# A fused two-layer kernel: u and v rows turned and moved apart with v first, the first pair's rows turned by TensorE, an earlier first gate, ScalarE in the opening normalisation, and two batches in one round of TensorE's loop

## The reference, cut to what matters

```python
xn = layernorm(x)
x = x + L0_attn(xn) + L0_ffn(xn)
xn = layernorm(x)
x = x + L1_attn(xn) + L1_ffn(xn)

def L0_attn(xn):                         # 16 channels of rank 64
    u, v = xn @ fu.T * s, xn @ fv.T * s  # (tokens, 16 x 64) each
    F = einsum("csr,ctr->cst", u, v); q = sigmoid(F)
    g1 = einsum("cst,ctr->csr", q, v); g2 = einsum("cst,csr->ctr", q, u)
    return (g1 @ fu + g2 @ fv) * s
```

## Time and profile before

| | |
|---|---|
| median of 3 runs | 1467.37 us (1465.08 to 1467.95) |
| the profiled execution | 1468.4 us, its span 1466.6 us |
| opening, router, experts | 0 to 158 us |
| batch 0, without layer 1 | 158 to 302 us |
| batches 1 to 7 of the loop | 302 to 1413.8 us |
| tail | 1413.8 to 1466.6 us |
| busy, of the span | PE 95%, DVE 62%, ACT 47%, POOL 3% |

### The profile page before, as it was taken

One profiled execution on the slowest core, in us unless ns is written; L12 is line 12 of the kernel. 1 busy time (PEld: TensorE's weight loads), 2 busy tenths in 40 slices (PEclk: granted clock), 3 DMA queues, 4 the chain that ended last, 5 costly groups with the idle time before them and its releaser, 6 DMA issues.

```text
span 1466.6 us, 24503 instructions
## 1 busy us (share of the span) xinstructions
PE 1389.9 (95%) x7806; PEld 793.9 (54%) x7806; DVE 903.6 (62%) x1559; ACT 688.9 (47%) x1058; POOL 44.1 (3%) x41
## 2 busy tenths in 40 slices
PE   6999798899998999999999999999999999999968
PEld 3566444455564555555565555555655555555534
DVE  8868443366655665656655656556555666566657
ACT  3556344444443544454444543454544454454421
POOL 4000400000000000000000000000000000000000
PEclk9999899999999999999999999999999999999988
DMA  6012222112221212221112211221212111221110
GB/s 207 1 31 66 43 35 31 26 29 35 30 30 31 33 27 30 36 32 31 26 26 39 36 29 24 36 34 28 30 29 36 32 26 27 38 30 27 25 30 8
DMA packets 302620, 51.37 MB, mean 35 GB/s; under 512 B 280545, under 2 KB 300769, under 8 KB 302465
## 3 DMA queue, kind: packets, MB, share of 16 engines
q1 hardware_dynamic: 302128, 47.82, 19.4%
q0 software_dynamic: 336, 1.64, 0.3%
HBM read 11.64 MB, written 4.19 MB: 11 GB/s over the span
## 4 chain that ended last, share of the span: by engine, by line
issue 85%; DVE 1%; PE 1%; POOL 1%; ACT 0%; POOLq 0%; DVEq 0%
PE psum L1231 1%; DVE arena L917 0%; DVE arena L923 0%; DVE arena L915 0%; POOL u_w_hl L608 0%; POOL v_w_hl L608 0%; POOL rstd_s L623 0%; POOL up_hl L608 0%; DVE arena L939 0%; PE psum L1575 0%; DVE xn_s L663 0%; POOL u_w_hl L605 0%; POOL v_w_hl L605 0%; DVE x_all L932 0%; POOL up_hl L605 0%
## 5 line engine op out<-in xcount | busy, mean ns | idle before, releaser
L1172 ACT ACTIVATE arena<-psum 128x1024 f32<-128x1024 f32 x504 | 476.0, 1030 | 636.5 <-PE psum L1231 636.3
L1231 PE MATMUL psum<-arena 128*64 128x512 f32 x2016 | 466.0, 605 | 26.0 <-DMA arena<-blocks 14.6
L1231 PEld LDWEIGHTS psum<-arena 128*64 128x64 f32 x2016 | 135.0, 138 | 290.0 <-issue 244.7
L1231 PE MATMUL psum<-u_parts,v_parts 64*128 64x512 f32 x1536 | 199.5, 404 | 11.9 <-issue 11.2
L1231 PE MATMUL psum<-v_parts,u_parts 64*128 64x512 f32 (+1 forms) x1568 | 201.9, 397 | 0.0
L866 DVE TENSOR_SCALAR o_hl<-psum,sums 128x512 fp32r<-128x512 f32 x126 | 94.4, 749 | 162.1 <-PE psum L1231 162.1
L1231 PEld LDWEIGHTS psum<-u_parts,v_parts 64*128 64x128 f32 x1536 | 141.7, 187 | 93.1 <-issue 45.3
L1231 PEld LDWEIGHTS psum<-v_parts,u_parts 64*128 64x128 f32 (+1 forms) x1568 | 145.3, 184 | 81.5 <-issue 51.1
L868 DVE SCALAR_TENSOR_TENSOR o_hl<-psum,sums,o_hl 128x512 fp32r<-128x512 f32 x126 | 94.6, 751 | 4.5
L1121 ACT ACTIVATE arena<-psum 128x512 f32<-128x512 f32 x128 | 77.1, 625 | 18.5 <-PE psum L1231 18.5
L923 DVE TENSOR_TENSOR arena<-psum,arena 128x512 f32<-128x512 f32 x96 | 64.6, 689 | 33.7 <-PE psum L1231 31.7
(11 more groups left out here) (211 smaller groups left out, 1517.0 us busy)
## 6 DMA issues: line engine op xcount, KB each, us to landing
arena<-blocks SPq DMA_DIRECT2D x1008, 32.0 KB, 2.0
x_all<-in_x SPq DMA_DIRECT2D x4, 512.0 KB, 5.4
upper<-in_we SPq DMA_DIRECT2D x8, 256.0 KB, 2.7
expert_rows<-upper SPq DMA_DIRECT2D x16, 128.0 KB, 2.5
xn_s<-expert_rows SPq DMA_DIRECT2D x8, 256.0 KB, 2.9
out<-x_all SPq DMA_DIRECT2D x8, 256.0 KB, 2.5
arena<-in_e POOLq DMA_DIRECT2D x1, 896.0 KB, 5.7
arena<-in_wi POOLq DMA_DIRECT2D x1, 576.0 KB, 5.7
```

The source lines that it names most:

```text
L1172: nc.scalar.activation(th_of(un), psum[:, at:at + 2], ACT.Tanh, scale=0.5 * FACTOR_SCALE ** 2).then_inc(s_th, 2)
L1231: return nc.tensor.matmul(out, lhsT, rhs, start=start, stop=stop)
```

## The change

Five edits.

1. **u and v apart, v first.** `turn` is called twice, for `v_raw` and then `u_raw`, 128x512 each, with buffers (`v_blocks`, `u_blocks`) and semaphores of their own. SP moves v with 16 DMAs of 16 KB and then u with 16 more, so 32 for a pair. `weighted` waits for v's at unit 0 and for u's only at unit 4 (half o = 1).
2. **First pair's rows by PE.** The turn of pair 1 of batch 0 and its 16 DMAs go; PE turns `u_raw` and `v_raw` with four transposes each (`prep` with k = 3 and 4), between the last expert's steps, and ACT copies the banks (`prep_tok`). PE now waits for these copies before its first scores (`s_prep_free` 8 in place of 6).
3. **First gate.** The steps gate 0 and up 0 move from half 5 to half 3, behind `v`; in the tail likewise.
4. **ACT's half of the opening.** ACT normalises every odd batch (`odd_rows`, four instructions of 128x128), DVE makes for it the shift and keeps the even ones. The router logits come in pairs of batches, two matmuls of 32 columns each, and the exponential is two instructions on 32 partitions each.
5. **Two batches a round on PE.** PE's loop `Fori(1, B)` becomes batch 1 written out and `Fori(1, B // 2)` with two batches in its body. DVE, ACT and SP keep one batch a round.

The core of the diff:

```diff
-FULL_STEPS = {1: [("back", 0)], 2: [("norm", 0)], 3: [("kq", 0), ("v", 0)], 12: [("down", 0)], 15: [("yo", 0), ("yo", 1)]}
-FULL_STEPS |= {h: [("gate", f), ("up", f)] for h, f in ((5, 0), (6, 1), (9, 2))}
+FULL_STEPS = {1: [("back", 0)], 2: [("norm", 0)], 3: [("kq", 0), ("v", 0), ("gate", 0), ("up", 0)], 12: [("down", 0)], 15: [("yo", 0), ("yo", 1)]}
+FULL_STEPS |= {h: [("gate", f), ("up", f)] for h, f in ((6, 1), (9, 2))}
...
+    return 3 + k if is_first(g) else g * 2 + 5 + k
+
+
+def moved_count(i, j):
+
+    return (i + (j > 0)) * MOVED
...
+            def move_blocks(blocks, tok, moved):
+
+                for r in range(QUARTERS):
+                    for a in range(QUARTERS):
+                        sp.dma_start(tok[32 * r:32 * r + 32, :, 32 * a:32 * a + 32],
+                                     blocks[32 * a:32 * a + 32].rearrange("t (k r c) -> t k r c", k=TB, r=QUARTERS)[:, :, r])\
+                          .then_inc(moved, 16)
+
+            def move_tokens(i, j):
+
+                sp.wait_ge(s_vb, i * PAIRS + j)
+                move_blocks(v_blocks, v_tok[:, (j + 1) % 2], s_vt[j])
+                sp.wait_ge(s_ub, i * PAIRS + j)
+                move_blocks(u_blocks, u_tok[:, (j + 1) % 2], s_ut[j])
+
             for j in range(1, PAIRS):
-                move_tokens(0, j, later_blocks)
+                move_tokens(0, j)
...
             def part_rows(h):
                 dve.wait_ge(s_rstd, h + 1)
-                for n in range(h * X_PART, (h + 1) * X_PART):
-                    if n >= 2:
-                        dve.wait_ge(s_xT, n - 1)
-                    normalised(xn_g[:, n % 2], n, mv1[:, n, :, 0:1], rstd1[:, n].unsqueeze(2)).then_inc(s_xn, 1)
+                odd, even = h * X_PART + 1, h * X_PART
+                nc.vector.scalar_tensor_tensor(shift1[:, odd], mv1[:, odd, :, 0], -1.0, rstd1[:, odd], ALU.mult, ALU.mult)\
+                  .then_inc(s_shift, 1)
+                if h:
+                    dve.wait_ge(s_xT, even - 1)
+                normalised(xn_g[:, 0], even, mv1[:, even, :, 0:1], rstd1[:, even].unsqueeze(2)).then_inc(s_xn, 1)
...
+            def turn(i, j, raw, blocks, turned, moved):
+
+                if not (isinstance(i, int) and i == 0 and j == 1):
+                    dve.wait_ge(moved[(j - 1) % PAIRS], moved_count(i if j else i - 1, (j - 1) % PAIRS))
+                nc.vector.transpose(blocks[:], raw[:]).then_inc(turned, 1)
...
-                        turn(i, j, later_blocks)
+                        turn(i, j, v_raw, v_blocks, s_vb, s_vt)
+                        turn(i, j, u_raw, u_blocks, s_ub, s_ut)
...
+            def odd_rows(n):
+                act.wait_ge(s_shift, n // 2 + 1)
+                if n >= 2:
+                    act.wait_ge(s_xT, n - 1)
+                for k in range(TB):
+                    ins = nc.scalar.activation(xn_g[:, 1, k], x_all[:, n, k], ACT.Identity, bias=shift1[:, n, k:k + 1],
+                                               scale=rstd1[:, n, k:k + 1])
+                ins.then_inc(s_xna, 1)
+
+            odd_rows(1)
+            for n in range(0, B, 2):
+                transposed(n, 0)
+                transposed(n + 1, 1)
+                if n + 3 < B:
+                    odd_rows(n + 3)
...
+            def prep_tok(k, tok, bk):
+                act.wait_ge(s_prep_full, prep_index(0, k) + 1)
+                copy(tok[:, 1].rearrange("p k c -> p (k c)"), bk[:]).then_inc(s_prep_free, 1)
...
+            prep_tok(3, u_tok, bank[2])
+            prep_tok(4, v_tok, bank[3])
...
+            def logits(pair):
+                pe.wait_ge(s_xnT, 2 * pair + 2)
+                for g in range(2):
+                    ins = mm(bank[2][g * 64:g * 64 + 32], wr_b[:, pair * 32:pair * 32 + 32], xn1T[:, 2 * pair + g],
+                             pair == 0, pair == B // 2 - 1)
+                return ins
...
+                else:
+
+                    pe.wait_ge(s_prep_free, prep_index(g, k - 2) + 1)
+                    for t in range(TB):
+                        ins = nc.tensor.transpose(bk[:, t * P:(t + 1) * P], (u_raw if k == 3 else v_raw)[:, t * P:(t + 1) * P],
+                                                  ident[:])
...
+                if blk == 0 and isinstance(i, int) and i == 0 and j == 1:
+                    pe.wait_ge(s_prep_free, prep_index(0, 4) + 1)
+                elif blk == 0:
+                    pe.wait_ge((s_vt, s_ut)[o][(j - 1) % PAIRS], moved_count(i if j else i - 1, (j - 1) % PAIRS))
...
             prep(0, 2, 1, 0, bank[1])
             probabilities_back(*last)
+            prep(0, 3, 1, 0, bank[2])
             attend(*last)
+            prep(0, 4, 1, 0, bank[3])
             expert_out(*last)
...
             iteration(0, True, False)
-            with pe.Fori(1, B) as i:
-                iteration(i, True, True)
+            iteration(1, True, True)
+            with pe.Fori(1, B // 2) as m:
+                for n in range(2):
+                    iteration(m * 2 + n, True, True)
             iteration(B, False, True)```

How the instructions stand, at the three places that matter. First SP, from the last expert to the first pairs of batch 0, before (`expert_rows<-upper` are the experts' stores, `xn_s<-expert_rows` their loads for the scatter):

```order
L514 DMA expert_rows<-upper 64x4x128 x4
L533 DMA arena<-arena 32x8x32 x16
L514 DMA expert_rows<-upper 64x4x128 x2
L542 DMA xn_s<-expert_rows 128x4x128
L533 DMA arena<-blocks 32x8x32 x32
L542 DMA xn_s<-expert_rows 128x4x128
L533 DMA arena<-blocks 32x8x32 x80
```

More of the change, by code:

```diff
@@ L231, in scatter_bank @@
         def scatter_bank(i):
-            return x_bank(("sc", 0), not isinstance(i, int))
+            return x_bank(("sc", 0), not (isinstance(i, int) and i == 0))
         x_all = sb("x_all", [P, B, TB, D])
@@ L375, in build @@
         w_hl = [u_w_hl, sb("v_w_hl", [P, 2, PAIRS * D], F32R)]
-        later_blocks = sb("blocks", [P, 2, T])
+        u_blocks, v_blocks = sb("u_blocks", [P, T]), sb("v_blocks", [P, T])
         def th_of(un):
@@ L1117, in prep_raw @@
                     act.wait_ge(s_us if k == 1 else s_vs_rdy, g + 1)
-                    act.wait_ge(s_turned, g)
+                    if isinstance(g, int) and g == 1:
+                        act.wait_ge(s_prep_full, prep_index(0, 4) + 1)
+                    else:
+                        act.wait_ge(s_ub if k == 1 else s_vb, g - 1)
                 if q is not None:
@@ L1233, in _, with transposes @@
             pe.wait_ge(s_first, 16 * len(first_consts))
-            def transposes(n, par):
-                pe.wait_ge(s_xn, n + 1)
-                if later(n):
+            def transposes(n):
+                par = n % 2
+                if par == 0:
+                    pe.wait_ge(s_xn, n // 2 + 1)
+                else:
+                    pe.wait_ge(s_xna, n // 2 + 1)
+                if n >= 2:
                     pe.wait_ge(s_xnT, n - 1)
@@ L1241, in transposes @@
                 ins.then_inc(s_xT, 1)
-            def logits(n):
-                pe.wait_ge(s_xnT, n + 1)
-                return mm(bank[2][0:E * B], wr_b[:, n * E * B:(n + 1) * E * B], xn1T[:, n], n == 0, n == B - 1)
-            transposes(0, 0)
-            pe.wait_ge(s_wr, 2)
-            for n in range(1, B):
-                transposes(n, n % 2)
-                logits(n - 1)
-            logits(B - 1).then_inc(s_lg, 1)
+            def logits(pair):
+                pe.wait_ge(s_xnT, 2 * pair + 2)
+                for g in range(2):
+                    ins = mm(bank[2][g * 64:g * 64 + 32], wr_b[:, pair * 32:pair * 32 + 32], xn1T[:, 2 * pair + g],
+                             pair == 0, pair == B // 2 - 1)
+                return ins
+            transposes(0)
+            transposes(1)
+            pe.wait_ge(s_wr, 2)
+            for n in range(2, B, 2):
+                transposes(n)
+                transposes(n + 1)
+                logits(n // 2 - 1)
+            logits(B // 2 - 1).then_inc(s_lg, 1)
             def early_prep(w, bk):
@@ L1472, in prep @@
                 pair = slice(j * P, (j + 1) * P)
-                if is_first(g):
+                if k in (1, 2) and is_first(g):
                     ins = mm(bk[:], (uT_w if k == 1 else vT_w)[:, pair], xn1T[:, 0])
-                else:
+                elif k in (1, 2):
                     if j == 0 and k == 1:
```

67 lines of the change are left out of this document (27 added, 40 removed).

## The result

| | before | changed | ratio, 95% interval |
|---|---|---|---|
| median, runs on one chip | 1466.22 us | 1570.05 us | 1.0705 [1.0686, 1.0723] |
| span of the profiled execution | 1466.6 | 1568.4 | |

The change costs 104 us. The forecast was 1432 us and faster. It lost to the second rival (1610): SP's queue became the bound. Its three signs are there: half moves at 0.6 us, SP without waits for the turns, batches above 170 us.

What follows compares the result with a forecast made beforehand. PE was taken as the bound, gains lying in its idle time: 2.5 + 7.7 + 9.3 + 8.0 + 2.3 + 8.5 = 38.3, less 3, gave 1433.1 us profiled, 1432 median. Its own range was 1424 to 1444; the range given reached 1475.

Steps and rivals of the forecast that it cites:

- the second rival: SP's queue becomes the bound: a half move costs 0.611 us, a loop batch takes 177, total 1610; chance 0.20.
- v first: Later pairs: v's moves land earlier, so PE's waits for moves go; 9.3 us in the loop, 8.0 in batch 0.
- the middle, 0.475: Price in us taken for issuing one half move on SP's queue, between 0.342 and 0.611.
- price by run: SP's issue cost follows the number of runs: `expert_rows` stores cost 0.616, just as the whole moves, both having 256 runs.
- price by partition: SP's issue: stores of x, 512 runs on 128 partitions, cost 0.404, so runs are cheap, fewer partitions dear.
- The upper bound: SP's issue of a half move saves nothing against a whole one: 0.611 us.
- The limit: SP's queue decides the time from where 32 moves fill 19.7 us less 1.1, 0.58 each, an issue of 0.54.
- the gain of 8.0: Batch 0: pairs go from 18.5 to SP's 17.6 us, 7 x 0.9, plus 1.7 for slow sums; bounds 0 and 9.
- Opening and first pair: Before the loop: exponential earlier by 2.5 us; first pair's move wait, slow sums and transpose waits save 7.7.
- Gate: Tail: gate and up fill PE's 2.68 us wait for `val_low`, 2.3 us gained; 0 in the loop.
- Two batches a round: PE's loop: four of six issue waits at round ends go, 7.3 us, plus 1.2 for the clock: 8.5 us.
- the cycle of turn and moves: Each pair's weighted sums, evacuation and turn, moves and landing: 19.1 us, predicted to fall to 16.6.

Runs made afterwards that it cites:

- m1: Standalone kernel without the reference work: groups of SP moves of varied partitions, runs and sizes, between buffers or via DRAM; issue prices only, no total time given.
- m2: Standalone kernel without the reference work: eight groups of 8 DMAs, on chip or with one end in DRAM; issue prices only, no total time given.
- a14: Changed kernel with 28 of the 32 half moves of a pair kept (14 of v, 14 of u): 1445.4 us, ratio 0.9879.
- a8: Changed kernel with half of the moves left out (8 of 16 for v, 8 of 16 for u): 1428.4 us, ratio 0.9756.
- a24: Kernel before with edits 2 and 4 alone: 1453.8 us, ratio 0.9915.
- POOL's half: Half of the 16 whole moves of a pair issued by POOL, edit 1 undone: 1431.5 us with two batches a round, 1433.6 with one.
- b5: Kernel before with edit 5 alone: 1471.2 us, ratio 1.0048.
- a1: Changed kernel with edit 1 alone undone: 1462.7 us, ratio 0.9977.
- p8: Changed kernel with edit 1 undone and 8 of the 16 whole moves of a pair issued by POOL: 1431.5 us, ratio 0.9773.
- the three parts alone: Kernel before with edits 2 and 4, with edit 3, and with edit 5, each put in separately: 1453.8, 1463.9 and 1471.2 us.
- b16: Kernel before with 16 extra 2 KB moves on SP's queue in each later pair: 1609.1 us, ratio 1.0985.
- d1: Changed kernel with edit 1 undone and the 16 moves replaced by 4 stores to and 4 loads from DRAM: 1558.8 us, ratio 1.0645.
- b1: Kernel before with edit 1 alone: 1618.3 us, ratio 1.1053.

## Why the prediction was wrong, point by point

**v first: the term that failed.** The step was "I take the middle, 0.475, being near neither row". The issue costs 0.601. The prediction weighed two explanations of the earlier trace rows, price by run and price by partition, and m1 and m2 bear out neither: both ends of these moves are on chip, and then an issue costs 0.59 to 0.62 with up to 256 runs, at 2 to 256 KB and 32 to 128 partitions. The rows at 0.34 and 0.40 had one end in DRAM, and in m2 the first issue of such a group is cheaper than the rest; in a row the store of x cost 0.80. The one row of the same way and engine was the whole move at 0.611, and nothing in the trace spoke for less than that by anything but a comparison across ways. The upper bound was the value to take. The rule of the Trainium skill cited there, that small transfers are mostly overhead and should be coalesced ("DMA: Bandwidth & Descriptors", "Rules for kernel authors"), said so, and the trace agrees, 2 KB costing what 32 KB costs.

**The limit.** The prediction put it at "an issue of 0.54". 28 issues of 0.60 fill a pair as 32 of 0.53 would, and a14 is free of the loss in the loop; 32 of 0.60 are not. The limit lies between, as worked out.

**The mechanism of v first** was right in the loop, given a cheap issue: in a14 v's 14 moves take 9.0 to 9.9 us (8.8 were forecast) and no wait for moves is left there. In batch 0 it was not: the gain of 8.0 was to come from pairs of 17.6 us, SP's part, and a14's pairs take 19.1, more than the 18.5 before, the time of SP's 28 issues, the longer ones among them, and the load of expert rows. That a8 came to 1428 says what an emptier queue gives, not that the forecast's 17.6 us a pair would have. With whole issues v's 16 moves take 10.3 us, as both tensors' did, so in the changed kernel v isn't earlier by anything but the shorter turn, and u comes 11 us later.

**The second rival's size.** It gave 1610; measured 1570. Its batch of 177 was 174.2, 20 us over seven. Of the other 20 the edits 2, 3 and 4 are 4 (14 measured, 10 counted); the rest was not taken apart.

**Opening and first pair**, 10.2 for 12.1 measured, the sum right and the parts less so: the exponential ends 1.8 us earlier for 2.5 in the changed kernel, the first weighted sums start 9.5 us earlier in a24 and then PE waits 2.4 for DVE, and half of the gain stands in the loop. **Gate**, 2.3 for 1.9 alone: right; its larger worth beside POOL's half isn't explained.

**Two batches a round**, 8.5, measured at 6 us slower by itself. The term's own sum, four waits of 1.8 us, is borne out where the cycle of turn and moves is short: beside POOL's half the four waits and 5.8 us of six batches go. It fails where that cycle stays at 19.1 of the 19.9 us of a pair: in b5 and a1 PE's saved time comes back as waits for moves, and a1 gains 3 us and not 19. The prediction had the cycle at 16.6 by v first, so this term rested on the failed one without saying so; a1's expectation took it over with the cycle at its old length. Two things stay open: why a longer round stopped PE twice in b5 (4.0 us) and once in a1 and p8 (1.4 and 1.8), and the 5 us by which a1 is slower than the three parts alone add up to (12.1 and 1.9 faster, 6.2 slower).

**The chances.** SP as the bound had 0.20. With two rows of 0.61 for moves to or from fewer partitions and none on chip below it, it deserved more than the forecast.

## What to carry to other kernels

Count DMA issues on a queue as instructions on an engine: number times price against the loop's period, before bytes are looked at; splitting a transfer in two doubles it. Where the trace has no row of the new shape, take the price from the row of the same way (on chip or DRAM) and not from one of like size. When a queue is the late one, a second engine that idles can issue half of it, and an engine's saved time is worth little while a cycle beside it is nearly as long.

## What the runs showed of the hardware

- An issue on SP's queue between two tiles on chip costs 0.59 to 0.62 us at 2 to 256 KB with up to 256 runs, 0.64 and 0.69 with 512 and 1024 runs (m1, m2, b16); with one end in DRAM 0.30 to 0.40 for a first one and 0.42 to 0.80 in a row (m2).
- POOL issues the same move in 0.582 us, and it lands in 2.0 us (p8).
- A store of 4 x 128 KB to DRAM is known to have landed some 6 us after its last issue, while a move on chip lands in 2.0 (d1).
- The end of a loop round stops PE 1.3 to 2.2 us with one batch in it, and 1.73 + 2.30 in one case with two (b5). The end of a round of SP's loop stops its queue 3.3 us in b1, 4.1 in b16 and 0.5 in the changed kernel.
- PE behind a wait of 3.31 us runs 16 sums in 5.35 us in place of 3.65, which adds to what a full queue costs (b1).
